# Attention: the masked keys of the second head parity move from ScalarE to GpSimd

## The reference, cut to what matters

```
B, H, W, C = 4, 112, 112, 128;  WIN = 8;  HEADS = 8;  HD = 16
q, k, v = windows of roll(x @ w_qkv + biases)          # 64 tokens a window
q = l2norm(q) * exp(scale)
k = l2norm(k)                                          # x * rsqrt(max(sum(x*x), 1.55e-5))
attn = softmax(q @ k.T + bias + shift_mask)            # per window and head
out  = (attn @ v) @ w_proj + b_proj
```

## Time and the profile before

| | us |
|---|---|
| median of three runs | 10792.27 |
| the three runs | 10792.55, 10792.27, 10772.9 |
| the profiled execution's own time | 10787.32 |
| its span in the trace | 10785.5 |
| the attention stage, from the first to the last step | about 1064 to 3142 |

### The profile page before, as it was taken

How to read it: one execution, slowest core, us unless ns; L and a number is a source line. 1 busy time by engine, 2 the same in 40 slices (tenths; PEclk the granted TensorE clock), 3 DMA queues, 4 the chain that set the end, 5 groups by cost and what they waited for, 6 DMA issues and landing times. The chain is left out here.

```text
span 10785.5 us, 111540 instructions
## 1 busy us (share of the span) xinstructions
PE 4563.0 (42%) x31813; PEld 2715.7 (25%) x31813; DVE 5474.9 (51%) x14162; ACT 3929.5 (36%) x9657; POOL 6184.6 (57%) x6259
## 2 busy tenths in 40 slices
PE   0011777777758997873222222223223223223000
PEld 0011555555544444541111111111111101101000
DVE  9987999999986775541121121121121112112487
ACT  0011888888854554332121111112112112112255
POOL 0000555555532224667777777777777777777675
PEclk9755999999978998876666666666666666666555
DMA  0000111111121223543222222222222222222366
GB/s 20 2 0 34 40 39 38 39 41 38 39 78 55 62 62 100 141 121 55 44 46 49 44 46 49 44 42 53 44 42 53 44 42 53 44 42 48 134 250 244
DMA packets 1326096, 663.81 MB, mean 62 GB/s; under 512 B 1058255, under 2 KB 1239100, under 8 KB 1320764
## 3 DMA queue, kind: packets, MB, share of 16 engines
q1 hardware_dynamic: 1142396, 576.49, 19.5%
q0 software_dynamic: 183104, 80.22, 5.7%
HBM read 344.86 MB, written 313.71 MB: 61 GB/s over the span
## 5 line engine op out<-in xcount | busy, mean ns | idle before, releaser
L1832 POOL DMA_INDIRECT gr_rec<-rec,gr_idx x4096 | 3954.2, 965 | 1248.8 <-issue 1248.0
L1853 PE MATMUL gr_p_h<-gr_tT,gr_w 128*128 128x512 f32 x1568 | 849.4, 696 | 3671.7 <-ACT gr_hT L1887 3638.7
L1972 DVE TENSOR_SCALAR gr_pen<-gr_same 128x64 f32<-128x64 f32 x64 | 13.7, 213 | 3170.6 <-DMA gr_rec<-rec,gr_idx 3170.6
L1853 PEld LDWEIGHTS gr_p_h<-gr_tT,gr_w 128*128 128x128 f32 x1568 | 347.6, 227 | 4154.9 <-ACT gr_hT L1887 3723.8
L544 POOL TENSOR_TENSOR at_sq<-at_qk 128x256 f32<-128x256 f32 x392 | 290.2, 740 | 1844.1 <-ACT at_qk L594 1843.9
L1900 ACT ACTIVATE gr_ee<-gr_dd 128x512 f32<-128x512 f32 x64 | 40.3, 629 | 3588.0 <-DVE gr_dd L1991 3588.0
L1858 PE MATMUL gr_p_y<-gr_hT,gr_w 128*128 128x512 f32 x1568 | 688.9, 592 | 0.0
L1952 DVE STREAM_TRANSPOSE gr_z<-gr_yb 128x2048 f32<-128x2048 f32 x98 | 226.5, 2311 | 902.8 <-issue 491.5
L1887 ACT ACTIVATE gr_hT<-gr_p_h,gr_b 128x512 f32<-128x512 f32 x784 | 517.6, 688 | 191.7 <-PE gr_p_h L1853 191.0
L2140 POOL DMA_INDIRECT cb_a<-scan,cb_idx x392 | 499.0, 1273 | 133.7 <-issue 122.4
L1340 POOL DMA_INDIRECT adst<-co_rec,co_idx x448 | 424.5, 948 | 223.3 <-issue 123.1
(11 more groups left out here) (358 smaller groups left out, 13212.1 us busy)
## 6 DMA issues: line engine op xcount, KB each, us to landing
y<-gr_z SPq DMA_DIRECT2D x392, 256.0 KB, 5.4
cb_y<-y SPq DMA_DIRECT2D x28, 3584.0 KB, 13.2
gr_rec<-rec,gr_idx POOLq DMA_INDIRECT x4096, 2.3
scan<-gr_out SPq DMA_DIRECT2D x64, 768.0 KB, 3.8
at_xs<-in_x_win SPq DMA_DIRECT2D x56, 448.0 KB, 3.8
x<-at_x SPq DMA_DIRECT2D x56, 448.0 KB, 4.2
ff_x<-x SPq DMA_DIRECT2D x56, 448.0 KB, 3.4
x<-ff_x SPq DMA_DIRECT2D x784, 32.0 KB
```

What stands on the lines that cost most here:

```text
L1832: nc.gpsimd.indirect_dma_start(out=rec[s][:, j, :], out_offset=None, in_=rec_dram, in_offset=bass.IndirectOffsetOnAxis(ap=idx[s][:, j:j + ...
L1853: nc.tensor.matmul(p_h[m % 4][:, :], w1[:, P * m:P * (m + 1)], tT[b.k][:, :], start=True, stop=True).then_inc(S["hp"], 1)
```

## The change

Of the two copies of the keys, ACT still writes the first (e = 0, semaphore kn). The second (e = 1) is written by POOL, as one `tensor_scalar` of 128 x 128 float32 from and to SBUF, with a semaphore of its own, kn2. In POOL's queue it stands behind at_sq and ahead of the gathers; it waits for at_qkn of pair t+2 (from DVE, in the same step) and for the scores of pair t (the buffer). PE's scores now wait for kn and kn2, and DVE's at_qkn waits for both before it writes its buffer again.

```diff
--- before.py
+++ after.py
@@ -392,7 +392,7 @@
 
         S = {n: sem(n) for n in (
             "consts_in", "setup", "ks", "beff_p", "x_in0", "x_in1", "x_out0", "x_out1", "xstat", "xrstd", "xb",
-            "xh", "xTp", "xT", "qkvp", "qk", "v", "sq", "norm", "rs", "qkn", "kn", "scores",
+            "xh", "xTp", "xT", "qkvp", "qk", "v", "sq", "norm", "rs", "qkn", "kn", "kn2", "scores",
             "logit", "prob", "pTp", "pT", "outp", "den", "oT", "proj", "x1", "dot", "wstat", "wrstd", "score", "passed", "passed_sp")}
         N = PAIRS
         HALF = 2 * PPS
@@ -505,6 +505,7 @@
 
                         r = p.slot(1)
                         p.wait("kn", 1)
+                        p.wait("kn2", 1)
                         p.wait("logit", 0, 3, 1)
                         p.wait("x1", -4)
                         for w in range(2):
@@ -542,6 +543,13 @@
                         p.wait("qk", 3)
                         p.wait("norm", 1)
                         nc.gpsimd.tensor_tensor(sq[r][:, :], qk[r][:, :], qk[r][:, :], ALU.mult).then_inc(S["sq"], 1)
+
+                    if p.has(2):
+                        r = p.slot(2)
+                        p.wait("qkn", 2)
+                        p.wait("scores", 0)
+                        nc.gpsimd.tensor_scalar(kn[r][:, :, 1, :], qkn[r][:, P:2 * P].rearrange("p (w k) -> p w k", w=2),
+                                                kscale[:, 2:3], None, ALU.mult).then_inc(S["kn2"], 1)
 
                     at, j = (p.i, p.u // PPS), p.u % PPS
                     if 0 <= p.u < HALF and j < 3:
@@ -620,10 +628,8 @@
                         r = p.slot(2)
                         p.wait("qkn", 2)
                         p.wait("scores", 0)
-                        for e in range(2):
-                            ins = nc.scalar.activation(kn[r][:, :, e, :], qkn[r][:, P:2 * P].rearrange("p (w k) -> p w k", w=2),
-                                                       ACT.Copy, scale=kscale[:, 1 + e:2 + e])
-                        ins.then_inc(S["kn"], 1)
+                        nc.scalar.activation(kn[r][:, :, 0, :], qkn[r][:, P:2 * P].rearrange("p (w k) -> p w k", w=2),
+                                             ACT.Copy, scale=kscale[:, 1:2]).then_inc(S["kn"], 1)
                     strip, s, j = p.strip(0)
                     if j == 2 and p.has(0) and p.has(PPS):
                         p.wait("xh", 4 - PPS)
@@ -721,6 +727,7 @@
                         p.wait("qk", 2)
                         p.wait("scores", 0)
                         p.wait("kn", 0)
+                        p.wait("kn2", 0)
                         nc.vector.scalar_tensor_tensor(qkn[r][:, :], rs[r][:, :], QK_EPS ** -0.5, qk[r][:, :], ALU.min, ALU.mult).then_inc(S["qkn"], 1)
                     strip, s, j = p.strip(0)
                     if j == 1 and p.has(0) and p.has(PPS):
```

## The result

The changed kernel takes 10850.52 us in the median of six runs (10843.46 to 10854.71), the kernel before, on the same chips, 10790.72 (10772.9 to 10792.55). The ratio is 1.0057, with a 95% interval from 1.0044 to 1.007: 60 us slower. I had said 10810, in a range from 10775 to 10870, with 0.42 for slower. The way was right; the size was three times mine, and near to the rival in which the GpSimd instruction is dear.

A forecast was written before the change was run, and what follows sets the result against it. VectorE was taken to bound the attention stage. The terms -8 (a), +17 (c), +17 (d) and -7 (e) sum to +19 us, 10811 as a median, said as 10810, in a range from 10775 to 10870.

The forecast's parts named there:

- What bounds the stage: Attention stage: VectorE, busy 93% of 2078.0 us, bounds it; ScalarE holds it about once in a round of 14 steps.
- (a): ScalarE makes one at_kn fewer; this counts only where at_rs is late behind the table load: -8 us.
- (b): GpSimd's new key instruction of 128 elements was put at 0.35 us, near to the copy's price.
- the 0.5 from which I had called the prediction wrong: Sign on GpSimd's new instruction: a row above 0.5 us makes the prediction wrong; 0.3 to 0.4 was expected.
- (c): GpSimd's queue: the new instruction waits for at_qkn ahead of the gathers, so edge_of's es_junk waits: +17 us, 0 to 50.
- the 0.43 that I took off: At edge_of's es_junk: at_sq gets out of the way during the wait, so 0.43 us come back, netting +0.5.
- (d): The new instruction delays VectorE's at_xb and es_junk in j = 3, the router's score in j = 4: +17 us.
- (e): at_sq starts earlier, leaves at_xb and at_qkn, meets at_xh and in some rounds the long es_junk: -7 us.
- The sum: All terms on the whole kernel: -8 + 17 + 17 - 7 = +19 us on 10787.3.
- My own range: Range of the +19 forecast for the whole kernel: -5 to +45 us, given a chance of 0.52.
- The dear rival: GpSimd's instruction takes 0.61 us, at_sq's price: +68 us, about 10860; chance 0.20.

The follow-up runs named there:

- behind_tt: behind, with GpSimd making the keys by tensor_tensor with a table of scales instead of tensor_scalar: 10833.72 us against 10789.45 for the kernel before, ratio 1.004.
- act_only: The kernel before with the second parity's keys left out (zero), no GpSimd work added: 10767.74 us, ratio 0.9984 to the kernel before.
- forms: The kernel before with 14 GpSimd instructions of several forms and sizes on scratch buffers ahead of the attention loop: 10796.84 us in one run.
- behind: The changed kernel with GpSimd's key instruction moved behind the gathers in its queue: 10789.86 us against 10784.65 for the kernel before, ratio 1.0006.
- wait_only: The kernel before, with GpSimd only waiting for at_qkn ahead of the gathers, no instruction there: 10845.71 us against 10784.65, ratio 1.006.
- wait_j6: The kernel before with the bare GpSimd wait ahead of the gathers in steps j = 6 alone: 10832.06 us against 10789.45, ratio 1.0038.
- wait_j4: The kernel before with the bare GpSimd wait ahead of the gathers in steps j = 4 alone: 10819.54 us, ratio 1.0028 to the kernel before.
- both: The changed kernel with ScalarE still making both keys and GpSimd writing into an unread buffer: 10854.36 us, ratio 1.0066 to the kernel before.
- behind_both: behind, with ScalarE making both keys and GpSimd writing into an unread buffer: 10850.17 us against 10802.52 for the kernel before, ratio 1.0044.
- no_table: The kernel before with ScalarE's function table loaded once, not again in each of 28 rounds: 10760.97 us against 10789.45, ratio 0.9973.

## Why the prediction was right in its way and short in its size

- **What bounds the stage**: right. In the table every kernel's stage follows what VectorE waits for and how it is stretched, but for at_junk in behind_tt; ScalarE, with 92 us less work, gave 8 at at_rs; another 11 went at at_oT and at_x, which had no term in the sum.
- **(a) ScalarE's relief, -8**: at_rs waits fell by 7.5. Alone it was worth 17 (act_only), so most of the half that I did not count lay at at_oT and at_x.
- **(b) The instruction's length, 0.35 us**: mis-sized; it is 0.603, above the 0.5 from which I had called the prediction wrong, and by that sign it is. I took the copy as the nearest row. That at_sq's undisturbed 612 ns fits is luck: it reads two inputs of 256 elements, and by the run forms neither half of it (0.31) nor a two-input instruction of 128 (0.45) is the price of tensor_scalar.
- **(c) The gathers, +17**: the mechanism is right (behind, wait_only, wait_j6), the size wrong: 61 us of waits. This is the term that failed, and its steps can be told apart. The first gather I put at 0.57 us after at_qkn (0.07, 0.35 and 0.15), and it starts at 0.87; 0.25 of the difference is the instruction's length. A shorter instruction would not have helped, since behind the bare wait it is 0.81. The gross wait at es_junk I had near in one strip of each round, 0.9 to 1.1 against 1.23 in the mean; in the other it is 0.40, not 0.1. What failed is the 0.43 that I took off: in the steps j = 0 es_junk's stretch fell from 7.3 to 3.6 us, but at_qkn's in front of it rose from 0.2 to 6.9, so at_sq gave nothing back. And I had looked at edge_of alone, while block_of waits 20.7 us for its own gathers, 17 more than before.
- **(d) The instruction against VectorE, +17**: too large. Of the places that I named the score's second instruction shows it, 168 ns before and 234 after in the mean, +3.7 us; at_xb and es_junk of 448 elements became shorter.
- **(e) The squares move, -7**: of the six instructions the four that I looked at are stretched 21 us less (at_xb 8.5, at_xh 5.5, at_qkn 4, es_junk of 448 elements 3), but the long es_junk 25 more, and at_lm, which I had not looked at, 11 more: at_sq runs beside all 66 of its lengthened records. So the squares' move is about +15, not -7. I had named that meeting and given it to "some rounds"; it happens in 30 of 56 steps, and wait_j4, where it happens in 47, is 30 us slower with no late gathers at VectorE.
- **The sum**, +19, was too small by its largest term: waits +61 in place of +17, stretch +15 in place of the +10 of (d) and (e), relief -8, and -11 at at_oT and at_x. Together that is +57 of the stage's +65. My own range for this sum, -5 to +45, does not hold the 60; the whole range does, by the rival alone.
- **The dear rival**, +68 at the price of at_sq, is near to the +60, but that is luck: it had +32 for the gathers and +51 for (d), where the runs show +61 and about +4, and the wait costs as much without the instruction. The point from which the rival decided, 0.5 us, was passed and did not matter to the queue.

## What to carry to other kernels

Before work is moved to an engine with room in its busy time, read what is queued behind the place: here a wait in front of DMA issues cost 61 us by itself, and with 392 instructions of 0.6 us behind the wait the loss was hardly larger (1.0066 in both, 1.006 in wait_only). An instruction that was put behind the DMA issues was not free either (behind_both). Put what waits for another engine behind what does not, and count how late the last DMA of each group lands. And look first at the largest wait of the engine that bounds: one line that reloads a table was worth more than all of the moved work.

## What the runs showed of the hardware

- A gather (DMA_INDIRECT) of GpSimd starts 0.16 to 0.17 us behind another GpSimd instruction, and 0.81 us behind a wait with nothing in between (wait_only). An instruction of 0.6 us put there is nearly hidden: 0.87 us (the changed kernel).
- GpSimd's tensor_scalar in float32 with a scalar per partition takes 358, 598 and 919 ns for 32, 128 and 256 elements (forms, undisturbed), which is 0.28 us and 2.5 ns an element, and tensor_tensor of 128 elements 0.45 us, less than tensor_scalar's 0.60 with its one tensor.
- The es_junk of 896 elements, of two SBUF inputs, whose record starts while a gather runs, with at_sq next in GpSimd's queue, ends 0.96 us after at_sq, though at_sq's record starts 0.33 us after its own: 1.91 instead of 1.08 us, and 1907 ns is the median of the 56 (wait_j4). That it is held until at_sq has ended is read from these times. "SBUF — State Buffer" of the Trainium skill, section "Who interferes with whom", gives the shared ports to whichever instruction issues first; by the start times in this trace the later one had them. The trace has starts and not issues, so it does not settle which came first. But the gather in front matters: in nine traces (before, after, wait_only, wait_j6, wait_j4, behind, both, act_only, no_table) I counted the cases in which this es_junk began at least 0.05 us before an at_sq that it met. It was lengthened in 157 of the 218 in which at_sq followed a gather directly, and in none of the 75 in which it did not.
